# Each engine's order in the Q and K stage with a step of slack, and attention scores and maxima for two heads at a time

## The chip, the cores and the metric

The kernel runs on one core of a Trainium2 chip. The metric is the device time of one execution in microseconds (us), as the median of several runs. The core has five engines that run their own instruction streams in order and meet only at semaphores: the tensor engine (PE, with its weight loads PEld), VectorE (DVE), ScalarE (ACT), GpSimd (POOL) and SyncE (SP), which here only issues DMAs.

## The reference

Input are x (4 x 512 x 512), a context (4 x 512 x 256) and two gates. First a selective scan (Mamba-like) runs over the context, gated by the normalized x, and is added to x; then a transformer block with causal attention (16 heads of 32) and a mixture of experts (8, two per token, and a shared one) runs over the normalized sum and is added again. Everything is float32. What matters here, cut down:

```python
def step(state, xs):                      # the scan: 512 channels, 16 states each, 512 steps
    d_t, B_t, C_t, u_t = xs
    dA = jnp.exp(d_t[..., None] * A)
    state = state * dA + (d_t * u_t)[..., None] * B_t[:, None, :]
    y_t = jnp.einsum('ben,bn->be', state, C_t)
    return (state, y_t)
...
q = (h @ wq + bq); k = (h @ wk + bk); v = (h @ wv + bv)      # as 16 heads of 32
q, k = _rope(q, k)
scores = jnp.einsum('bqhd,bkhd->bhqk', q, k) * HEAD_DIM ** (-0.5)
attn = jax.nn.softmax(jnp.where(causal[None, None], scores, min), axis=-1)
ctx = jnp.einsum('bhqk,bkhd->bqhd', attn, v)
x = x + ctx @ wo
```

## The kernel before

The work goes in rounds, `round_(b, s)` on each engine, with b the batch whose attention runs and s = b + 1 the batch whose scan runs: a first round with the scan of batch 0 alone (to some 205 us), three rounds with both (to some 497, 793 and 1087 us), and a last one with the attention of batch 3 alone (to 1286 us). Then the experts' stage runs to the end; the change doesn't touch it.

**The scan.** It is cut into 64 blocks k of 128 channels x 512 positions: state n = k // 4, channel tile et = k % 4. GpSimd makes GB = DU x BB (`driven(k)`, four buffers), ScalarE the decay exp(A delta) in a PSUM bank (`decay(k)`), VectorE the scan itself (`scan(k)`), which writes row n into one of two buffers: `even_states` for even n, `xa` for odd n. So row n writes over row n - 2, and `scan(4n)` waits until the turns of all blocks up to 4n - 5 are done (`hT_ready`). The tensor engine turns a finished block of 128 positions (`turn_states(q)`, four transposes into a bank), and VectorE adds it, times C, to the output sum YA (`add_state(q)`). In the Q and K stage two banks take the turned states by turns, in the attention loop only HT0 does: there each turn waits for the sum before it.

**The Q and K stage** has eight steps m. Step m makes one of eight tiles of Q or K: `product` (twelve matmuls of 128x512, a product of split numbers) and `rotate` (the rope's swap, a matmul) on the tensor engine, `bias` on ScalarE, `rope_cos` on GpSimd (writes RC, two buffers), `rope_out` on VectorE (two operations, RS and then QK from RC and RS). Beside it two blocks of the scan go through in each step.

**The attention loop** has sixteen steps q: row tile i = q // 4, four heads m = q % 4, tiles 128 x W with W = 128 (i + 1). The tensor engine makes the scores of four heads one q ahead (`scores(q + 1)`), VectorE their negated maxima (`row_max`), ScalarE the exponentials (`probs`, one per head), the tensor engine transposes each (`turn`), ScalarE copies it out (`keep_turned`, PT), and `weigh(q)` multiplies with V behind a transpose of the inverse sums (`rib`). The three blocks of the scan k = 16 + 3q, k + 1, k + 2 go beside it, with three turned and summed states. `finish` (the product with wo, the second norm, the router) of row tile i - 1 is spread over the q of tile i.

All orders are written out by hand, in `round_` of each engine. One PSUM area SB of four banks holds the scores; the same banks are A[0] to A[3], which the rotation (A[0], A[1]), the turned states (A[2]) and the decays (A[3]) use in the Q and K stage.

## Time and profile before

| | |
|---|---|
| median of 3 runs | 2016.72 us (2014.46 to 2017.73) |
| the profiled execution | 2015.7 us, span 2013.9 us |
| mean granted clock of the tensor engine | 0.845 of full speed |
| busy: PE, DVE, ACT, POOL | 1560.5, 1174.1, 887.6, 808.3 us |
| chain that ended last, by engine | PE 51%, issue 18%, DVE 8%, POOL 7%, ACT 5% |

The profile is one execution of the program. Busy times are sums over the span, which has stages with different limits, so they are read stage by stage. In the chain of waits "issue" is time in which an engine waited for nothing that the profile shows. A matmul's own duration overlaps the next one's; the distance from start to start tells what it costs.

### The profile page before, as it was taken

What the parts mean: (1) busy time and instruction counts of PE and PEld (TensorE: products, weight loads), DVE (VectorE), ACT (ScalarE), POOL (GpSimd) and SP (SyncE); (2) the same over time, 40 slices, a digit from 0 to 9 for tenths busy, and PEclk for the clock granted to TensorE, in tenths of its full rate; (3) what the DMA queues carried; (4) which work ended last, traced back from release to release, by engine and by line L of the source; (5) the groups of instructions that cost most, each with busy time, mean ns of one, the idle gap of its engine ahead of it and who ended that gap; (6) DMA issues with size and microseconds to landing.
All of it is one profiled execution on the core that took longest, in us unless ns stands there. A gap on an engine that the chain in (4) does not pass through costs nothing.

```text
span 2013.9 us, 26645 instructions
## 1 busy us (share of the span) xinstructions
PE 1560.5 (77%) x9104; PEld 1196.1 (59%) x9104; DVE 1174.1 (58%) x1730; ACT 887.6 (44%) x1973; POOL 808.3 (40%) x809
## 2 busy tenths in 40 slices
PE   5345866776866777767776877789999999999994
PEld 2234543554544555544554644677878799999973
DVE  4779657777557777557775334233233365666545
ACT  5342624664524665515663256211111266666610
POOL 0685145443145542244542212123522265555544
PEclk8555975788985888986788878899999999999997
DMA  5521000112100112000112200542211187777564
GB/s 196 212 65 63 12 16 21 48 49 68 32 16 21 59 42 74 28 12 30 43 37 63 79 22 33 214 179 81 92 52 37 46 299 258 254 246 252 171 239 157
DMA packets 95109, 197.31 MB, mean 98 GB/s; under 512 B 9008, under 2 KB 25904, under 8 KB 91648
## 3 DMA queue, kind: packets, MB, share of 16 engines
q1 hardware_dynamic: 89856, 178.83, 25.8%
q0 software_dynamic: 5120, 16.78, 2.5%
q8 instruction: 74, 1.21, 0.2%
q14 instruction: 59, 0.48, 0.1%
HBM read 141.97 MB, written 53.61 MB: 97 GB/s over the span
## 4 chain that ended last, share of the span: by engine, by line
PE 51%; issue 18%; DVE 8%; POOL 7%; ACT 5%; DMA 0%; DVEq 0%; ACTq 0%; POOLq 0%; SPq 0%
PE scores L552 20%; PE bank L552 13%; PE bank L628 4%; PE scores L692 3%; PE bank L705 3%; DVE YA L1444 3%; POOL GB L1860 3%; PE bank L720 3%; ACT PT L1100 2%; POOL yab L2013 2%; ACT EX L1092 1%; PE scores L695 1%; DVE nm L1505 1%; PE bank L716 1%; PE bank L881 1%
## 5 line engine op out<-in xcount | busy, mean ns | idle before, releaser
L1860 POOL TENSOR_TENSOR GB<-DU,BB 128x512 f32<-128x512 f32 x256 | 324.2, 1290 | 48.8 <-DVE DL L1415 21.6
L1056 ACT ACTIVATE bank<-DL,aneg 128x512 f32<-128x512 f32 x200 | 138.0, 690 | 159.3 <-DVE xa L1434 94.1
L1100 ACT ACTIVATE PT<-bank 128x128 f32<-128x128 f32 (+3 forms) x256 | 111.0, 434 | 146.4 <-PE bank L705 143.1
L1444 DVE SCALAR_TENSOR_TENSOR YA<-bank,Ct,YA 128x512 f32<-128x512 f32 x208 | 153.1, 737 | 13.8 <-PE bank L628 10.8
L552 PE MATMUL scores<-xth,wgh 128*128 128x256 f32 x552 | 158.0, 286 | 2.2 <-DVE fa L1747 1.1
L628 PE MATMUL bank<-ident,xa 128*128 128x128 f32 x432 | 90.9, 350 | 85.9 <-DVE YA L1444 60.7
L628 PE MATMUL bank<-ident,even_states 128*128 128x128 f32 x400 | 81.7, 340 | 97.5 <-DVE even_states L1434 53.4
L552 PE MATMUL scores<-xth,wgl 128*128 128x256 f32 x552 | 156.1, 283 | 0.0
L552 PE MATMUL scores<-xtl,wgh 128*128 128x256 f32 x552 | 156.0, 283 | 0.0
L705 PE MATMUL bank<-ident,EX 128*128 128x128 f32 x640 | 133.1, 316 | 17.6 <-ACT PT L1100 15.8
L1092 ACT ACTIVATE EX<-scores,nm 128x128 f32<-128x128 f32 (+3 forms) x256 | 133.6, 523 | 23.6 <-DVE nm L1505 23.0
L1434 DVE TENSOR_TENSOR_SCAN xa<-bank,GB 128x512 f32<-128x512 f32 x100 | 121.9, 1219 | 17.9 <-ACT bank L1056 17.6
L1434 DVE TENSOR_TENSOR_SCAN even_states<-bank,GB 128x512 f32<-128x512 f32 x100 | 121.9, 1219 | 17.8 <-ACT bank L1056 17.7
L628 PEld LDWEIGHTS bank<-ident,even_states 128*128 128x128 f32 x400 | 56.6, 173 | 125.5 <-DVE even_states L1434 64.8
L628 PEld LDWEIGHTS bank<-ident,xa 128*128 128x128 f32 x432 | 63.7, 178 | 110.3 <-DVE YA L1444 61.0
L1985 POOL TENSOR_TENSOR fal<-fa,fah 128x512 fp32r<-128x512 f32 x36 | 46.5, 1290 | 200.3 <-ACT fah L1268 200.1
L552 PE MATMUL scores<-hah,wgh 128*128 128x512 f32 x320 | 125.6, 392 | 1.1 <-DVE lg L1535 1.1
L552 PE MATMUL scores<-hal,wgh 128*128 128x512 f32 x320 | 125.3, 392 | 0.0
L552 PE MATMUL scores<-hah,wgl 128*128 128x512 f32 x320 | 125.2, 391 | 0.0
L1968 POOL TENSOR_TENSOR wgl<-wgr,wgh 128x768 fp32r<-128x768 f32 x54 | 110.6, 2050 | 30.4 <-ACT wgh L1239 30.4
L1892 POOL TENSOR_TENSOR PT<-EX,rope 128x512 f32<-128x512 f32 x32 | 41.9, 1309 | 197.8 <-ACT EX L1084 197.8
L1505 DVE TENSOR_REDUCE nm<-scores 128x4 f32<-128x512 f32 (+3 forms) x64 | 95.3, 1489 | 34.4 <-PE scores L695 33.8
(250 smaller groups left out, 4108.4 us busy)
## 6 DMA issues: line engine op xcount, KB each, us to landing
wgr<-wffn_in SPq DMA_DIRECT2D x108, 384.0 KB, 6.3
wdr<-wffn_in SPq DMA_DIRECT2D x81, 256.0 KB, 3.4
BB<-b_scratch SPq DMA_DIRECT2D x64, 256.0 KB, 3.1
xg<-V SPq DMA_DIRECT2D x1, 11776.0 KB, 39.0
xr<-xg SPq DMA_DIRECT2D x23, 512.0 KB, 5.8
yg<-ysb SPq DMA_DIRECT2D x23, 512.0 KB, 6.3
hah<-hhd SPq DMA_DIRECT2D x5, 1024.0 KB, 6.0
hal<-hhd SPq DMA_DIRECT2D x5, 1024.0 KB, 8.3
```

The source lines that it names most:

```text
L552: mm = nc.tensor.matmul(out_, parts[a](k), rhs_parts[b](k), start=(k == 0 and j == 0), stop=(k == n - 1 and j == 2))
L628: mm = nc.tensor.transpose(into[:, et * P:(et + 1) * P], states(s, n)[:, et, tt * P:(tt + 1) * P], ident[:])
L692: nc.tensor.matmul(SB[:, a, 0:W], QK[r:r + HD, m, i * P:(i + 1) * P], QK[r:r + HD, 4 + m, 0:W], start=True, stop=False)
L705: mm = nc.tensor.transpose(turned_bank(b, v)[:, kb * P:(kb + 1) * P], EX[:, a, kb * P:(kb + 1) * P], ident[:])
L1056: nc.scalar.activation(into, DL[:, et, :], ACT.Exp, scale=aneg[:, et, n:n + 1]).then_inc(dA_ready, 1)
L1092: nc.scalar.activation(EX[:, a, 0:W], SB[:, a, 0:W], ACT.Exp, bias=nm[:, a:a + 1], accum_out=rs[:, q % 2, a:a + 1]).then_inc(ex_done, 1)
L1100: nc.scalar.activation(PT[:, a, 0:W], turned_bank(b, v)[:, 0:W], ACT.Copy).then_inc(pt_done, 1)
L1434: nc.vector.tensor_tensor_scan(states(s, n)[:, et, :], decay_bank(s, k)[0], GB[:, k % 4, :], 0.0, ALU.mult, ALU.add).then_inc(scan_done, 1)
L1444: nc.vector.scalar_tensor_tensor(YA[:, tt, :], state_bank(s, q)[0], Ct[:, tt, n:n + 1], YA[:, tt, :], ALU.mult, ALU.add).then_inc(y_acc, 1)
L1505: nc.vector.tensor_reduce(nm[:], SB[:, :, 0:W], AX.X, ALU.max, negate=True).then_inc(mx_done, 1)
L1860: nc.gpsimd.tensor_tensor(GB[:, k % 4, :], DU[:, et, :], BB[:, n % 2, :], ALU.mult).then_inc(gb_ready, 1)
L1968: nc.gpsimd.tensor_tensor(wgl[raw][:, c, :], wgr[raw][:, c * 2 * EW:(c + 1) * 2 * EW], wgh[raw][:, c, :].bitcast(f32), ALU.subtract).then_ ...
```

## The change

The numbers SL = 11 and NP = 2 NQ are new. In the Q and K stage:
- GpSimd makes the GB of blocks 0 and 1 first, and in step m those of 2m + 2 and 2m + 3 behind `rope_cos(m)` (2m and 2m + 1 before).
- VectorE runs `rope_out(m - 1)` at the end of step m, behind both scans (`rope_out(m)` between them before), and adds state k - 5 behind scan k (k - 4 before).
- The tensor engine puts `rotate(m - 1)` between the two turned states (ahead of both before) and turns eleven states in the stage (twelve before).

In the attention loop the scores and their maxima are made for two heads at a time: p = 2q + h. `scores(2q + 3)` stands where `scores(q + 1)` stood, `scores(2q + 4)` behind the third turned state of q. The turned states and their sums are one block later than before: 11 + 3q + a in q (12 + 3q + a before). The last one goes behind the loop.

```diff
@@ state_bank
-            if s == 0 or q < SQ - T4:
+            if s == 0 or q < SL:
                 return (HT0, A[2])[q % 2], q - 2
-            return HT0, q - 2 if q == SQ - T4 else q - 1
+            return HT0, q - 1
@@ tensor engine
-            def scores(b, q):
+            def scores(b, p):
+
+                q, h = divmod(p, 2)
                 i, m = quad(q)
                 W = P * (i + 1)
-                if q == 0:
+                if p == 0:
                     pe.wait_ge(v_done, T4 * b + T4)
                     pe.wait_ge(qk_done, 8 * b + 8)
-                    if b + 1 < B:
-                        pe.wait_ge(scan_done, NB * (b + 1) + SQ)
-                        pe.wait_ge(y_acc, NB * (b + 1) + SQ - T4)
-                at(pe, ex_done, UN * b + HG * q)
-                for a in range(HG):
+                if p == 1 and b + 1 < B:
+                    pe.wait_ge(scan_done, NB * (b + 1) + SQ)
+                    pe.wait_ge(y_acc, NB * (b + 1) + SL - 1)
+                at(pe, ex_done, UN * b + HG * (q - 1) + 2 * h + 2)
+                for a in (2 * h, 2 * h + 1):
...
                     if att:
                         product(b, m)
-                        if m:
-                            rotate(b, m - 1)
                     if scn and m >= 2:
                         turn_states(s, 2 * m - 4)
+                    if att and m:
+                        rotate(b, m - 1)
+                    if scn and 2 <= m < 7:
                         turn_states(s, 2 * m - 3)
                 if att:
                     rotate(b, 7)
                     scores(b, 0)
+                    scores(b, 1)
+                    scores(b, 2)
                 for q in range(NQ):
                     i, m = quad(q)
                     if att and q + 1 < NQ:
-                        scores(b, q + 1)
+                        scores(b, 2 * q + 3)
                     for a in range(HG):
+                        if att and a == 3 and q + 2 < NQ:
+                            scores(b, 2 * q + 4)
                         if att:
                             turn(b, HG * q + a)
                         if scn and a < SU:
-                            turn_states(s, SQ - T4 + SU * q + a)
+                            turn_states(s, SL + SU * q + a)
...
                 if scn:
+                    turn_states(s, NB - 5)
@@ ScalarE
-                act.wait_ge(mx_done, NQ * b + q + 1)
+                act.wait_ge(mx_done, NP * b + 2 * q + a // 2 + 1)
@@ VectorE
             def scan_out(s):
+                add_state(s, NB - 5)
...
-            def row_max(b, q):
+            def row_max(b, p):
+                q, h = divmod(p, 2)
                 W = P * (quad(q)[0] + 1)
-                dve.wait_ge(s_mm, NQ * b + q + 1)
-                nc.vector.tensor_reduce(nm[:], SB[:, :, 0:W], AX.X, ALU.max, negate=True).then_inc(mx_done, 1)
+                dve.wait_ge(s_mm, NP * b + p + 1)
+                nc.vector.tensor_reduce(nm[:, 2 * h:2 * h + 2], SB[:, 2 * h:2 * h + 2, 0:W], AX.X, ALU.max, negate=True
+                                        ).then_inc(mx_done, 1)
...
-                    if scn:
-                        scan_block(s, 2 * m)
-                    if att:
-                        rope_out(b, m)
-                    if scn:
-                        scan_block(s, 2 * m + 1)
+                    for k in (2 * m, 2 * m + 1):
+                        if scn:
+                            scan(s, k)
+                        if scn and k >= 5:
+                            add_state(s, k - 5)
+                    if att and m:
+                        rope_out(b, m - 1)
+                if att:
+                    rope_out(b, 7)
                 if att:
                     row_max(b, 0)
+                    row_max(b, 1)
+                    row_max(b, 2)
                     invert(b, 0)
...
                     if more:
-                        row_max(b, q + 1)
+                        row_max(b, 2 * q + 3)
                     if scn:
+                        add_state(s, k - 5)
+                        scan(s, k + 1)
                         add_state(s, k - 4)
-                        scan_block(s, k + 1)
                     if att and i and m != 1:
                         finish(b, i - 1, (1, 0, 2, 3)[m])
+                    if att and q + 2 < NQ:
+                        row_max(b, 2 * q + 4)
                     if scn:
-                        scan_block(s, k + 2)
+                        scan(s, k + 2)
+                        add_state(s, k - 3)
@@ GpSimd
+                if scn:
+                    driven(s, 0)
+                    driven(s, 1)
                 for m in range(8):
                     if att:
                         rope_cos(b, m)
                     if scn:
-                        driven(s, 2 * m)
-                        driven(s, 2 * m + 1)
-                if scn:
-                    driven(s, SQ)
-                    driven(s, SQ + 1)
+                        driven(s, 2 * m + 2)
+                        driven(s, 2 * m + 3)
```

VectorE at the start of the Q and K stage (round 0), before: even_states or xa is a scan, EX<-scores,rope and QK are the rope, YA a state's sum.

```order
L1434 SCALAR_TENSOR_TENSOR even_states<-scores,GB 128x512
L1495 SCALAR_TENSOR_TENSOR EX<-scores,rope 128x512
L1499 SCALAR_TENSOR_TENSOR QK<-PT,EX 128x512
L1434 SCALAR_TENSOR_TENSOR even_states<-bank7,GB 128x512
L1434 SCALAR_TENSOR_TENSOR even_states<-scores,GB 128x512
L1495 SCALAR_TENSOR_TENSOR EX<-scores,rope 128x512
L1499 SCALAR_TENSOR_TENSOR QK<-PT,EX 128x512
L1434 SCALAR_TENSOR_TENSOR even_states<-bank7,GB 128x512
L1434 SCALAR_TENSOR_TENSOR xa<-scores,GB 128x512
L1444 SCALAR_TENSOR_TENSOR YA<-bank6,Ct,YA 128x512
```

The same place in the changed kernel:

```order
L1444 SCALAR_TENSOR_TENSOR even_states<-scores,GB 128x512
L1444 SCALAR_TENSOR_TENSOR even_states<-bank7,GB 128x512
L1444 SCALAR_TENSOR_TENSOR even_states<-scores,GB 128x512
L1444 SCALAR_TENSOR_TENSOR even_states<-bank7,GB 128x512
L1501 SCALAR_TENSOR_TENSOR EX<-scores,rope 128x512
L1505 SCALAR_TENSOR_TENSOR QK<-PT,EX 128x512
L1444 SCALAR_TENSOR_TENSOR xa<-scores,GB 128x512
L1444 SCALAR_TENSOR_TENSOR xa<-bank7,GB 128x512
L1454 SCALAR_TENSOR_TENSOR YA<-bank6,Ct,YA 128x512
```

The rope of a tile has moved from between its step's scans to behind the next step's, and the first sum to behind scan 5.

VectorE in one q of the attention loop (q = 1, W = 128; nm is the maximum, ri the inverse, cn the context), before:

```order
L1434 SCALAR_TENSOR_TENSOR even_states<-bank7,GB 128x512
L1515 TENSOR_TENSOR cn<-bank4,rbs 128x128
L1505 TENSOR_REDUCE nm<-scores 128x4
L1444 SCALAR_TENSOR_TENSOR YA<-bank6,Ct,YA 128x512
L1434 SCALAR_TENSOR_TENSOR xa<-bank7,GB 128x512
L1444 SCALAR_TENSOR_TENSOR YA<-bank6,Ct,YA 128x512
L1434 SCALAR_TENSOR_TENSOR xa<-bank7,GB 128x512
L1444 SCALAR_TENSOR_TENSOR YA<-bank6,Ct,YA 128x512
L1510 RECIPROCAL ri<-rs 128x4
```

And in the changed kernel:

```order
L1444 SCALAR_TENSOR_TENSOR even_states<-bank7,GB 128x512
L1523 TENSOR_TENSOR cn<-bank4,rbs 128x128
L1512 TENSOR_REDUCE nm<-scores 128x2
L1454 SCALAR_TENSOR_TENSOR YA<-bank6,Ct,YA 128x512
L1444 SCALAR_TENSOR_TENSOR xa<-bank7,GB 128x512
L1454 SCALAR_TENSOR_TENSOR YA<-bank6,Ct,YA 128x512
L1512 TENSOR_REDUCE nm<-scores 128x2
L1444 SCALAR_TENSOR_TENSOR xa<-bank7,GB 128x512
L1454 SCALAR_TENSOR_TENSOR YA<-bank6,Ct,YA 128x512
L1518 RECIPROCAL ri<-rs 128x4
```

The one maximum of four heads has become two of two heads, and the second stands ahead of the q's third scan and sum. The first scan of xa here is block 20, the first of row n = 5: it writes over row 3, whose last block is now the second turned state of this q.

The tensor engine in the same q of the changed kernel (scores<-QK and maskb are the scores, bank5 the transposes of EX, bank6 the turned states, rib and V the sum over V):

```order
L696 MATMUL scores<-QK 128x128 x2
L699 MATMUL scores<-maskb,identb 128x128 x2
L709 MATMUL bank5<-ident,EX 128x128
L630 MATMUL bank6<-ident,xa 128x128 x4
L709 MATMUL bank5<-ident,EX 128x128
L630 MATMUL bank6<-ident,xa 128x128 x4
L709 MATMUL bank5<-ident,EX 128x128
L630 MATMUL bank6<-ident,even_states 128x128 x4
L696 MATMUL scores<-QK 128x128 x2
L699 MATMUL scores<-maskb,identb 128x128 x2
L709 MATMUL bank5<-ident,EX 128x128
L720 MATMUL bank4<-ident,rib 128x128
```

Before, the scores of four heads stood first in q; now two heads stand there and two behind the third turned state.

## Rows read from the trace of the kernel before

**Rows 1.** Sums by stage: window, length, busy us of each engine, granted clock, DMA.

```profile
545.00:605.00 60.00, 36.24 (x132) 24.90 (x130) 32.21 (x38) 13.92 (x21) 26.10 (x21) 0.82 0.05 14
605.00:791.00 186.00, 135.69 (x1016) 93.23 (x1016) 138.18 (x175) 105.90 (x289) 82.89 (x95) 0.75 0.16 49
```

**Rows 2.** Chain of waits, Q and K stage: start, us, what.

```profile
552.68 2.50 POOL GB L1860 x2
...
596.13 2.56 POOL GB L1860 x2
```

**Rows 3.** Timeline of one step: start, us, engine, line, operation, out<-in.

```profile
589.17 1.22 DVE L1434 TENSOR_TENSOR_SCAN even_states<-scores,GB 128x512 f32<-128x512 f32 x1 [3.35 <-POOL GB L1860]
590.31 0.73 DVE L1444 SCALAR_TENSOR_TENSOR YA<-bank,Ct,YA 128x512 f32<-128x512 f32 x1
...
590.95 0.68 DVE L1495 SCALAR_TENSOR_TENSOR EX<-scores,rope 128x512 f32<-128x512 f32 x1
591.66 0.69 DVE L1499 SCALAR_TENSOR_TENSOR QK<-PT,EX 128x512 f32<-128x512 f32 x1
592.27 1.22 DVE L1434 TENSOR_TENSOR_SCAN even_states<-bank,GB 128x512 f32<-128x512 f32 x1
...
593.52 0.69 ACT L1056 ACTIVATE bank<-DL,aneg 128x512 f32<-128x512 f32 x1 [2.41 <-DVE even_states L1434]
...
594.90 1.28 POOL L1892 TENSOR_TENSOR PT<-EX,rope 128x512 f32<-128x512 f32 x1 [4.53 <-ACT EX L1084]
```

**Rows 4.** Timeline: a rotation, a turned state; chain: a product.

```profile
599.04 1.02 PE L678 MATMUL scores<-EX,perm 128*128 128x512 f32 x2
...
599.90 0.60 PE L628 MATMUL bank<-ident,even_states 128*128 128x128 f32 x4
...
1123.77 2.75 PE bank L552 x12
```

**Rows 5.** Timeline of VectorE: the last sum of DL.

```profile
542.44 0.69 DVE L1415 TENSOR_TENSOR DL<-DL,GB 128x512 f32<-128x512 f32 x1
```

**Rows 6.** Timeline of rounds 3 and 0; line L1499: count, ns min/median/max.

```profile
1138.13 1.29 POOL L1892 TENSOR_TENSOR PT<-EX,rope 128x512 f32<-128x512 f32 x1 [2.31 <-ACT EX L1084]
...
1138.95 1.01 DVE L1499 SCALAR_TENSOR_TENSOR QK<-PT,EX 128x512 f32<-128x512 f32 x1
...
306.11 6.22 POOL L1860 TENSOR_TENSOR GB<-DU,BB 128x512 f32<-128x512 f32 x5
...
309.94 2.94 DVE L1499 SCALAR_TENSOR_TENSOR QK<-PT,EX 128x512 f32<-128x512 f32 x1
...
L1499 DVE SCALAR_TENSOR_TENSOR QK<-PT,EX x32: 691/693/2944, 249.2 to 1144.2; 128x512 f32<-128x512 f32 x32
```

**Rows 7.** Timeline of the tensor engine: the first scores.

```profile
612.82 0.81 PE L692 MATMUL scores<-QK 32*128 32x128 f32 x8 [7.09 <-DVE YA L1444]
```

**Rows 8.** Timeline: inverses turned, q = 0, 3, 15; thirteen left out.

```profile
623.91 0.47 PE L716 MATMUL bank<-ident,rib 128*128 128x128 f32 x1 [0.37 <-ACT PT L1100]
...
648.59 0.47 PE L716 MATMUL bank<-ident,rib 128*128 128x128 f32 x1 [0.37 <-ACT PT L1100]
...
778.45 0.43 PE L716 MATMUL bank<-ident,rib 128*128 128x128 f32 x1 [0.69 <-ACT PT L1100]
```

**Rows 9.** Chain of waits in q = 1: a turn, a sum.

```profile
628.32 1.10 PE bank L628 x4
...
629.52 0.76 DVE YA L1444
```

**Rows 10.** Groups by line, shapes apart: maxima (busy us, mean ns).

```profile
L1505 DVE TENSOR_REDUCE nm<-scores 128x4 f32<-128x2048 f32 x16 | 36.6, 2287 | 11.7 <-PE scores L695 11.7
...
L1505 DVE TENSOR_REDUCE nm<-scores 128x4 f32<-128x512 f32 x16 | 11.1, 692 | 8.6 <-PE scores L695 8.4
```

**Rows 11.** Chain of waits in round 3, W = 384: the maximum.

```profile
1218.40 1.77 DVE nm L1505
```

**Rows 12.** DMA issues of the page: count, KB each, us to landing.

```profile
BB<-b_scratch SPq DMA_DIRECT2D x64, 256.0 KB, 3.1
```

More of the change, by code:

```diff
@@ L34 @@
 SU = 3
+SL = 11
+NP = 2 * NQ
 MASKED = -3.0e38
@@ L693, in scores @@
                                      start=True, stop=False)
-                for a in range(HG):
+                for a in (2 * h, 2 * h + 1):
                     mm = nc.tensor.matmul(SB[:, a, W - P:W], identb[:], maskb[:], start=False, stop=True)
@@ L1445, in add_state @@
                                                ALU.mult, ALU.add).then_inc(y_acc, 1)
-            def scan_block(s, k):
-                scan(s, k)
-                if k >= T4:
-                    add_state(s, k - T4)
             def gate(s, tt):
```

## Prediction

> **What bounds the kernel now.** I read the sums by stage first. In one of the three rounds that hold both scan and attention, the Q and K stage takes 60 us with VectorE busy 32 of them and the tensor engine 36, and the attention loop 186 with 138 and 136 [rows 1]. No engine is full, so orders and waits set the time. Next the chain of waits: in the Q and K stage it comes back to GpSimd's pair of GB products once in each step m, and five steps last from 552.68 to 596.13, 8.69 each [rows 2]. The timeline of one step shows the ring [rows 3]. VectorE runs scan (589.17), sum, the two operations of the rope, scan (592.27); the second scan frees its bank for ScalarE's decay (593.52), behind which stands the bias of step m+1; that releases GpSimd's cosine product (594.90), behind which stand the GB products (596.13 in [rows 2]), for which VectorE's next scan waits. Only the written order ties these together: bias(m+1) stands behind decay(2m+3), and cosine(m+1) ahead of the GB products of the same step.
>
> **Q and K stage, in three rounds.** GpSimd now makes GB a step ahead, VectorE takes the rope a step later and adds each state one block later, and TensorE puts one turn between product and rotation. The ring of 8.69 opens, and what is left is each engine's own work in a step. VectorE, from start to start [rows 3]: scan 1.14, sum 0.64, scan 1.14, sum 0.64, rope 0.71 and 0.61, so 4.9. TensorE at full clock: product 2.75, rotation 0.86, two turns of 0.60 at most [rows 4], so 4.8. GpSimd: 1.23 + 2.56, so 3.8 [rows 2, 3]. About 5 a step, set by VectorE.
>
> One cost rises. The rope's last operation (QK<-PT,EX) has both its inputs in SBUF. Started during one cosine product it took 1.01 instead of 0.69; during five GB products in a row 2.94, until just after the last of them [rows 3, 6]. GpSimd now runs cosine, GB, GB without a gap in every step, so in my schedule a QK that falls into such a run waits for its end. Cosine(m+1) in its turn waits for QK(m-1), which keeps most of them apart. The schedule of one round, by hand from the rows: the last sum of DL starts at 542.44 and ends at 543.1 [rows 5]. GpSimd's first GB follows, loses some 0.5 to VectorE's last DU product (two SBUF inputs too) and ends at 545.0. Five GB and two cosines behind it, 1.26 each, end at 553.8; QK(0) waits for them and ends at 554.4. From there VectorE still has 12 scans (13.7), 11 sums (7.1) and 7 ropes (9.3), 30.1, and QK is held five times for 0.3 to 1.35, 2.9 together. QK(7) ends at 587.4 and the first scores can start; before, they start at 612.82, released by a sum of YA [rows 7]. **Gain 25.4 a round.** With no hold it is 29. With a hold as long as the worst row (2.94 - 0.69 = 2.25) in each of seven steps, 15.8 stands in place of 2.9, and it is 12.5. I take 25.4, since the median of all 32 is 0.69 [rows 6] and cosine cannot run ahead of QK by more than two.
>
> The Trainium skill, SBUF — State Buffer, "Who interferes with whom", says that a VectorE instruction with two SBUF inputs and a GpSimd one that reads SBUF exclude each other, and that the second fully blocks until the first finishes. The 1.01 row agrees with it; the 2.94 row goes further than one instruction. Held by one instruction only, QK(0) and QK(6) would end 1.2 to 1.3 sooner, and the time would be some 7 us lower.
>
> The loads of b rows (3.1 us to land [rows 12]) wait for the GB products of two rows before; they come earlier with them and have two steps in hand, so 0.
>
> **Attention loop, in three rounds.** Before, a q of the first four costs (648.59 - 623.91)/3 = 8.2, the next twelve 129.9 together [rows 8]. A q is paced by turn 1.10, sum 0.75, turn, sum, turn [rows 9], at half clock (the same four transposes took 0.60 [rows 4]); the scans run beside the turns. Three things add waits.
> (a) VectorE has row_max(2q+4) ahead of scan(k+2), and TensorE makes these scores only behind the third turn. The third scan no longer lies beside that turn: after it come half the scores (0.64), a maximum (0.43: widths differ by 0.53 for each 512 elements [rows 10]), scan 1.14, sum 0.75, inverse 0.15, scan 1.14, context 0.27, maximum 0.43, sum 0.7, turn, sum, turn (3.0): 8.7 against 8.2.
> (b) A state is turned one block later (SL = 11, where it was 12). scan(4n) writes over row n-2, so it waits for turn 4n-5. That was always a turn of the q before or one that a sum ahead had waited for. Now it is the first turn of the same q (q = 0, 4, 8, 12), the second (1, 5, 9, 13) or the third (2, 6, 10, 14, already in (a)). Price 0.7 to 1.1 for the second; 0 to 1.6 for the first, which has half the scores, a turn of EX, PT and the sum over V ahead of it.
> (c) Where a q also holds the product with wo (twelve matmuls, up to 2.75 as in [rows 4]), the third turn, its scores and the maximum stand behind it: about 1 more.
> Against these: the maximum ahead of the first sum is half as long, at 512 columns 1.2 instead of 2.29 [rows 10], and the first two exponentials of q+1 find theirs ready. My sums: entry 0.3, q 1 to 3 1.6 + 0.5 + 0.4, so +2.8; q 4 to 7 +2.8; q 8 to 11 +0.5; q 12 to 15 -1.0; one more turn behind the last sum over V +0.4. **Together +5.5 a round.** The ends: every wait at half clock +16; at full clock, hidden by the shorter maxima, -4. I take the value between, as the granted clock was 0.75 in this loop [rows 1].
>
> **Round 3, attention alone.** Its Q and K stage keeps its order. In the loop, a q whose chain held scores, the maximum (1.77 [rows 11]) and then four exponentials now has half the scores ahead, the rest before the fourth turn, and two exponentials that wait for nothing: 8.0 becomes 7.2 in the five q of that kind, and nothing where ScalarE's exponentials bound already. **-4**, between -10 and +3.
>
> **The first round, scan alone,** adds each state one block later; VectorE has the same operations and no wait: 0. The experts' stage is untouched: 0.
>
> **Sum.** 3 x (-25.4 + 5.5) - 4 = -63.7. On the profiled execution of 2015.7 (span 2013.9) that is 1952; the median of the runs lies 1.0 higher: 1953.
>
> **Rivals.**
> 1. The attention's new waits are covered, since the tensor engine runs more of it at full clock: -3 a round instead of +5.5, 3 x (-25.4 - 3) - 4 = -89, so 1927. For: with wide tiles VectorE's maximum led the chain, and it is halved. Against: the first q ran at half clock.
> 2. The holds or the waits come at their upper end. GpSimd is first every time: gain 12.5 instead of 25.4, 1953 + 39 = 1992. Or the waits cost +16 instead of +5.5: 1984. For: the 2.94 row. Against: cosine waits for the QK before last.
> 3. Slower than before: the tensor engine is granted 1.2 GHz through both stages. A step is then twice 4.8, so 9.6 against 8.69, no gain; and the loop costs +16: 2017 + 48 = 2065, anything from 2021 up. It decides once a step is over 6.7 (a gain under 16). Against: the old stage had 0.82 with the engine busy 36 of 60 us [rows 1]; it will be busy 4.8 of 5.
> 4. The ring opens but another one of the same length stands behind it, so the orders don't bring what they could: loops that I find take 4.2 (decay, bias, cosine, GB to the scan after next) and 4.3 (scan, sum, turn, product, turn, rotation, rope over two steps), both below 5. 2017 within 4.
>
> **How the numbers follow.** The forecast 1953 (1938 to 1968) has 50%; rival 1 18%; rival 2 24% (1968 to 2012); rival 3 5%; rival 4 3%. To hold 8 in 10 the range takes the forecast, rival 1 down to 1925 and rival 2 up to 1990. Faster by over 0.2% (about what a measurement can tell from no change) 92%, within it 3%, slower 5%.
>
> **What would show it.** GB pairs in the Q and K stage 5.0 to 5.6 apart, the granted clock above 0.9 there, the first scores some 45 us after the last sum of DL instead of 70, QK operations of 0.7 to 3 us; in the loop VectorE idle ahead of row_max for the scores and ahead of the first scan of a row for a turn, with q 1 near 9.8 and q 2 and 3 near 8.7. Wrong if the steps stay above 6.7, or if q 1 costs no more than q 2, or if the loop as a whole is longer by over 16.

## The result

The changed kernel takes 2034.43 us (median of 4 runs, 2032.09 to 2036.22), the kernel before 2015.59 beside it (4 runs, 2013.92 to 2017.73): ratio 1.0092, interval 1.0075 to 1.0110. It is slower by 19 us, where 1953 was forecast. The profiled execution has a span of 2034.4 us (2013.9 before) and a mean granted clock of 0.822 (0.845 before). One other execution of the kernel before, beside e1 to e4 below, took 2589.91 us at a granted clock of 0.543 and stands in no ratio.

Sums by stage, round 1 of the changed kernel. Columns as in [rows 1]: window, length, busy us of PE, PEld, DVE, ACT and POOL, granted clock, DMA. The first line is the Q and K stage, the second the attention loop:

```profile
540.00:588.00 48.00, 34.90 (x150) 24.35 (x150) 44.68 (x51) 19.99 (x31) 34.88 (x27) 0.96 0.08 23
588.00:785.00 197.00, 153.96 (x970) 101.53 (x970) 124.97 (x173) 104.69 (x287) 75.58 (x89) 0.68 0.12 37
```

The same stages of the kernel before, cut at its own first scores:

```profile
541.00:613.00 72.00, 39.64 (x144) 26.53 (x144) 40.94 (x49) 16.90 (x27) 34.66 (x27) 0.80 0.06 15
613.00:780.00 167.00, 123.83 (x956) 85.06 (x960) 123.84 (x155) 103.14 (x284) 75.50 (x88) 0.76 0.13 41
```

The Q and K stage lost 24 us and VectorE fills 93% of it. The loop grew by 30 us between these cuts, and so did the tensor engine's busy time in it: 154 against 124, with the clock at 0.68 against 0.76. VectorE's work in the loop is the same (125 and 124). So the gain came, and more than it went again in the loop.

Timeline around the end of the Q and K stage and the first scores (columns as in [rows 3]), to be set beside [rows 7]:

```profile
586.67 1.06 DVE L1505 SCALAR_TENSOR_TENSOR QK<-PT,EX 128x512 f32<-128x512 f32 x1
587.83 0.49 PE L696 MATMUL scores<-QK 32*128 32x128 f32 x4 [4.76 <-issue]
```

The inverses turned in q = 0, 3 and 15 of the same round, to be set beside [rows 8]:

```profile
600.38 0.47 PE L720 MATMUL bank<-ident,rib 128*128 128x128 f32 x1 [0.37 <-ACT PT L1110]
...
630.08 0.47 PE L720 MATMUL bank<-ident,rib 128*128 128x128 f32 x1 [0.37 <-ACT PT L1110]
...
782.08 0.33 PE L720 MATMUL bank<-ident,rib 128*128 128x128 f32 x1 [0.69 <-ACT PT L1110]
```

From q = 0 to q = 15 that is 181.7 us; before it was 154.5 [rows 8]. There is one such row for each q, so the distance between two of them is the price of a q. This table is worked out from all of them, in round 1 (for e1 and e6 too); the q meant is the later one:

| q | 1 | 2 | 3 | 4 | 5 | 6 | 7 | 8 | 9 | 10 | 11 | 12 | 13 | 14 | 15 | sum |
|---|---|---|---|---|---|---|---|---|---|---|---|---|---|---|---|---|
| before | 8.1 | 8.1 | 8.5 | 9.9 | 8.9 | 9.0 | 11.8 | 11.6 | 9.9 | 10.6 | 12.6 | 13.5 | 11.1 | 12.0 | 8.9 | 154.5 |
| after | 10.2 | 9.5 | 10.0 | 13.6 | 10.9 | 10.4 | 13.5 | 15.7 | 11.9 | 11.4 | 14.3 | 17.6 | 11.9 | 11.9 | 8.9 | 181.7 |
| e1, below | 9.1 | 7.5 | 8.5 | 14.1 | 9.7 | 9.0 | 11.6 | 17.2 | 10.8 | 10.6 | 12.3 | 18.5 | 12.0 | 12.4 | 8.9 | 172.1 |
| e6, below | 9.2 | 8.1 | 8.5 | 10.6 | 9.6 | 9.0 | 11.6 | 12.2 | 10.8 | 10.6 | 11.6 | 13.9 | 11.5 | 12.4 | 9.7 | 159.2 |

Over the whole kernel these rows give the account. The first inverse comes 23.5 us earlier (325.53 to 302.07), the stretches from a round's last inverse to the next round's first are shorter by 26.0 and 24.0 (142.4 to 116.4, 142.2 to 118.2): -73.5. The loops of the three rounds are longer by 25.9, 27.2 and 30.1, that of round 3 by 7.7 (115.4 to 123.1): +90.9. With +0.6 between rounds 2 and 3 the last inverse comes 18 us later (1267.1 to 1285.3). The rest of the kernel, which has the same instructions, takes 749.1 in this execution against 746.8.

### The profile page after: what moved, and what is told of

The parts are those of the page before. It is cut to its first block, busy times and chain, and to the rows that moved or that the text cites. A ratio compares the mean times of both kernels' runs of the same rounds, so it can differ in the third digit from the quotient of the medians.

```text
span 2034.4 us, 26709 instructions
## 1 busy us (share of the span) xinstructions
PE 1653.3 (81%) x9104; PEld 1238.7 (61%) x9104; DVE 1183.8 (58%) x1794; ACT 891.7 (44%) x1973; POOL 809.6 (40%) x809
## 4 chain that ended last, share of the span: by engine, by line
PE 60%; issue 11%; DVE 10%; ACT 4%; POOL 4%; DMA 0%; DVEq 0%; ACTq 0%; SPq 0%; POOLq 0%
PE scores L554 22%; PE bank L554 14%; PE scores L696 6%; PE bank L630 5%; DVE YA L1454 3%; PE bank L709 3%; PE bank L724 3%; PE scores L699 2%; ACT PT L1110 2%; POOL yab L2030 2%; DVE even_states L1444 1%; PE bank L720 1%; DVE xa L1444 1%; PE bank L891 1%; ACT EX L1102 1%
## 5 line engine op out<-in xcount | busy, mean ns | idle before, releaser
L1512 DVE TENSOR_REDUCE nm<-scores 128x2 f32<-128x256 f32 (+3 forms) x128 | 105.1, 821 | 129.3 <-PE scores L699 129.2
L696 PE MATMUL scores<-QK 32*128 32x256 f32 (+3 forms) x512 | 146.6, 661 | 23.7 <-issue 11.6
L1454 DVE SCALAR_TENSOR_TENSOR YA<-bank,Ct,YA 128x512 f32<-128x512 f32 x211 | 154.7, 734 | 13.9 <-PE bank L630 11.8
L630 PE MATMUL bank<-ident,even_states 128*128 128x128 f32 x412 | 89.3, 356 | 89.8 <-DVE YA L1454 64.0
L554 PE MATMUL scores<-xtl,wgh 128*128 128x256 f32 x552 | 156.0, 283 | 0.0
L709 PE MATMUL bank<-ident,EX 128*128 128x128 f32 x640 | 145.4, 340 | 8.6 <-ACT PT L1110 8.4
L630 PE MATMUL bank<-ident,xa 128*128 128x128 f32 x432 | 95.6, 365 | 57.3 <-DVE YA L1454 56.8
L630 PEld LDWEIGHTS bank<-ident,even_states 128*128 128x128 f32 x412 | 62.1, 181 | 112.1 <-DVE YA L1454 43.0
L2002 POOL TENSOR_TENSOR fal<-fa,fah 128x512 fp32r<-128x512 f32 x36 | 46.5, 1290 | 200.2 <-ACT fah L1278 200.0
L630 PEld LDWEIGHTS bank<-ident,xa 128*128 128x128 f32 x432 | 68.2, 187 | 78.6 <-DVE YA L1454 41.6
```

The costliest lines, as they stand in the source:

```text
L554: mm = nc.tensor.matmul(out_, parts[a](k), rhs_parts[b](k), start=(k == 0 and j == 0), stop=(k == n - 1 and j == 2))
L630: mm = nc.tensor.transpose(into[:, et * P:(et + 1) * P], states(s, n)[:, et, tt * P:(tt + 1) * P], ident[:])
L696: nc.tensor.matmul(SB[:, a, 0:W], QK[r:r + HD, m, i * P:(i + 1) * P], QK[r:r + HD, 4 + m, 0:W], start=True, stop=False)
L709: mm = nc.tensor.transpose(turned_bank(b, v)[:, kb * P:(kb + 1) * P], EX[:, a, kb * P:(kb + 1) * P], ident[:])
L1454: nc.vector.scalar_tensor_tensor(YA[:, tt, :], state_bank(s, q)[0], Ct[:, tt, n:n + 1], YA[:, tt, :], ALU.mult, ALU.add).then_inc(y_acc, 1)
L1512: nc.vector.tensor_reduce(nm[:, 2 * h:2 * h + 2], SB[:, 2 * h:2 * h + 2, 0:W], AX.X, ALU.max, negate=True).then_inc(mx_done, 1)
```

## The experiments

Three things stand mixed in the change: the orders of the Q and K stage, one block less between a turned state and the scan that writes over it (SL = 11, twelve before), and scores and maxima for two heads at a time. The first four kernels take them apart. The kernel before beside them took 2017.9, 2017.1 and 2016.0 us in the three groups of runs (e1 to e4; e5, e6, e8, e9; e7, e10, e11).

**e1: the stage's orders and SL = 11, four heads at a time.** Against the changed kernel:

```diff
-                        scores(b, 2 * q + 3)
+                        scores(b, q + 1)
...
-                        if att and a == 3 and q + 2 < NQ:
-                            scores(b, 2 * q + 4)
...
-                        row_max(b, 2 * q + 3)
+                        row_max(b, q + 1)
...
-                    if att and q + 2 < NQ:
-                        row_max(b, 2 * q + 4)
```

> The changed kernel with scores and maxima of four heads at a time again, at their old places; the new orders of the Q and K stage and the turned states one block later (SL = 11) stay. Theory A (two heads' scores occupy the tensor engine as long as four, since four heads' matmuls on 32 rows each run side by side; the pairs cost the attention loop its 26 to 30 us a round): the loop from the first to the last inverse turned goes back to within 5 to 9 of the old 156, that is the row waits alone, and the time is about 1965. Theory B (the waits of scan(4n) for a turn of the same q are the loss, at 1.0 to 2 us in half of the q): the loop stays at 170 or more and the time is 2000 or more.

Measured: 1998.50 us, ratio 0.9911 (0.9894 to 0.9929). The loops of the three rounds with both take 171.4, 172.1 and 173.2 us, so it is theory B that fits, the waits for a turn. Theory A, which had put nearly all of the loss on the scores, is out as to size by 33 us.

**e2: e1 with twelve states turned in the stage.** The attention loop is word for word that of the kernel before:

```diff
-SL = 11
+SL = 12
...
+                if scn:
+                    add_state(s, 11)
                 if att:
                     rope_out(b, 7)
...
-                        add_state(s, k - 5)
-                        scan(s, k + 1)
                         add_state(s, k - 4)
+                        scan(s, k + 1)
+                        add_state(s, k - 3)
```

> As the run before, and twelve turned states in the Q and K stage again (the twelfth sum between the last two ropes), so that the attention loop is that of the kernel before, word for word. Both theories: the loop takes 152 to 156 a round again, the Q and K stage keeps its gain of 24 less 0.7 for the sum, and the time is 2015.6 - 3 x 23.5 = 1945. If it is above 1965, the gain of the stage is given back by the attention loop for another reason than these orders (the state in which it starts).

Measured: 1938.32 us, ratio 0.9614 (0.9597 to 0.9631), 7 less than expected. The orders of the Q and K stage are worth 79.6 us alone, 26.5 a round. The one block of lead costs 60.2 (e1 against e2), some 19 in each of these loops (172.1 against 152.5 in round 1) and 3.9 ahead of the first inverse.

**e3: the kernel before with scores and maxima for two heads**, placed as in the changed kernel, and nothing else:

```diff
-                        scores(b, q + 1)
+                        scores(b, 2 * q + 3)
                     for a in range(HG):
+                        if att and a == 3 and q + 2 < NQ:
+                            scores(b, 2 * q + 4)
...
-                        row_max(b, q + 1)
+                        row_max(b, 2 * q + 3)
...
+                    if att and q + 2 < NQ:
+                        row_max(b, 2 * q + 4)
                     if scn:
                         scan_block(s, k + 2)
```

> The kernel before with the scores and maxima for two heads at a time alone (places as in the changed kernel; Q and K stage and turned states as before). Theory A: the loop takes 18 to 25 more in each of three rounds and 8 in the last, the time is 2015.6 + 60 to 85, about 2085. Theory B: only the third scan behind the second maximum, 0.6 in the first q and nothing later: about 2020, at most 2030.

Measured: 2055.27 us, ratio 1.0186 (1.0168 to 1.0204). Two heads at a time cost 37 us on their own, which neither theory had: A said 60 to 85, B at most 15. The loops are longer by 10.9, 10.8 and 15.6, that of round 3 by 7.7.

**e4: the kernel before, its score matmuls written in two halves in their old place.** The same matmuls, waits and maxima; only the order of the twelve records of one group changes:

```diff
-                for a in range(HG):
-                    r = HD * a
-                    nc.tensor.matmul(SB[:, a, 0:W], ...)
-                for a in range(HG):
-                    mm = nc.tensor.matmul(SB[:, a, W - P:W], identb[:], maskb[:], start=False, stop=True)
+                for h in range(2):
+                    for a in (2 * h, 2 * h + 1):
+                        r = HD * a
+                        nc.tensor.matmul(SB[:, a, 0:W], ...)
+                    for a in (2 * h, 2 * h + 1):
+                        mm = nc.tensor.matmul(SB[:, a, W - P:W], identb[:], maskb[:], start=False, stop=True)
```

> The kernel before; only the sequence of matmuls within the scores of four heads differs: heads 0 and 1, their masks, heads 2 and 3, their masks. Same matmuls, same waits, same places. Theory A: the scores of a q take twice 0.8 to 2.0 instead of once, about 1.2 more on average for 64 q and nearly all on the path: 2060 to 2095. Theory B, and any explanation by waits: no change, within 4 of 2015.6.

Measured: 2085.06 us, ratio 1.0338 (1.0316 to 1.0360): +67 for a change of order alone, as theory A said (2060 to 2095), where theory B had no change. Timeline of the tensor engine at 512 columns, first the kernel before, at half and at full clock (start, us; x8 are eight records, two for each of four heads):

```profile
734.79 2.09 PE L692 MATMUL scores<-QK 32*128 32x512 f32 x8
736.81 0.61 PE L695 MATMUL scores<-maskb,identb 128*128 128x128 bf16 x4
...
747.68 1.14 PE L692 MATMUL scores<-QK 32*128 32x512 f32 x8
748.75 0.40 PE L695 MATMUL scores<-maskb,identb 128*128 128x128 bf16 x4
```

The same in e4:

```profile
771.45 1.13 PE L693 MATMUL scores<-QK 32*128 32x512 f32 x4
772.51 0.28 PE L696 MATMUL scores<-maskb,identb 128*128 128x128 bf16 x2
...
782.32 2.08 PE L693 MATMUL scores<-QK 32*128 32x512 f32 x4
784.33 0.39 PE L696 MATMUL scores<-maskb,identb 128*128 128x128 bf16 x2
784.65 2.08 PE L693 MATMUL scores<-QK 32*128 32x512 f32 x4
786.66 0.39 PE L696 MATMUL scores<-maskb,identb 128*128 128x128 bf16 x2
```

The granted clock is 0.50 around the rows of 2.08 and 2.09 us and 1.00 around those of 1.13 and 1.14. At half clock four heads take 2.09 us and two heads 2.08. A head has 32 rows ("32*128" in the row), and the kernel takes those of head a from partition 32a on, so the four stand in different groups of rows, and they run together. Two of them alone are no sooner done.

**e7: one head at a time**, score and mask, score and mask:

```diff
                     nc.tensor.matmul(SB[:, a, 0:W], ...)
-                for a in range(HG):
                     mm = nc.tensor.matmul(SB[:, a, W - P:W], identb[:], maskb[:], start=False, stop=True)
```

> The kernel before, with the score matmuls and the mask of one head at a time: score 0, mask 0, score 1, mask 1 and so on. The same matmuls, waits and maxima. In e4 (heads 0 and 1 with their masks, then heads 2 and 3) the kernel before went from 2018 to 2085, +67. Theory: a group of score matmuls takes as long as one matmul, however many heads of 32 rows lie side by side in it, up to four. Four groups are two more than in e4, so another 2 x 67: near 2218, and the first of the four scores to the last mask twice as long as in e4. Rival: two heads side by side are already served one after the other, and what e4 cost is a fixed price of the change between scores and masks: with three changes more instead of one, 67 for each gives the same 2218, but then the trace shows scores of e4's pairs that start as far apart as in e7. If only a fixed latency is paid once, 2085 to 2100.

Measured: 2264.34 us, ratio 1.1247 (1.1219 to 1.1275), +181 and +248 against e4 and before. Timeline of the tensor engine at full clock:

```profile
867.50 1.12 PE L692 MATMUL scores<-QK 32*128 32x512 f32 x2
868.56 0.23 PE L694 MATMUL scores<-maskb,identb 128*128 128x128 bf16 x1
868.72 1.12 PE L692 MATMUL scores<-QK 32*128 32x512 f32 x2
```

One head takes 1.12, two 1.13, four 1.14: the time belongs to the group and not to the heads, and the rival of this expectation (two heads already served one after the other) is out. The busy time of all score matmuls, summed over the four widths of the view by line and shape, is 76 us before, 151 in e4 and 312 in e7, that of the masks 34, 46 and 70. That is +87 and +272 of busy time for +67 and +248 of time. The theory's size was short, 2264 for some 2218: a further group costs the engine much the same (87 us in e4, 272 / 3 = 91 in e7). Of the 87 in e4 20 don't show in the time, of the 272 in e7 24; a likely reason is that they lay in time that the engine waited anyway and that there was little more of it to fill, which no run tests.

The Trainium skill, TensorE: Matmul & The Clock Gate, "Part 3: Packing small matmuls — row/col tiling", says that small matmuls on different groups of 32 rows run at the same time, and gives 3.07 times the speed for four of them at 512 columns. These rows agree that they run together, and the factor by them is higher: 4 x 1.12 in e7 against 1.14 before, 3.9.

**e5: the changed kernel with twelve states turned in the stage** (the edit of e2 on top of the change).

> The changed kernel with twelve turned states in the Q and K stage and the attention's turned states and sums where they were before (lead of 12); the scores and maxima for two heads stay. Theory C (the two losses, pairs +37 and one block less of lead +60, are separate): 1938 + 37 = 1975. Theory D (they are one wait seen twice, scan and maximum behind the same turn): the pairs cost the less when the lead is back, under 1960, or the more, over 1990.

Measured: 1984.81 us, ratio 0.9839 (0.9822 to 0.9855), 10 above what theory C said and under the 1990 of theory D, so it settles neither. The lead is worth 49.6 here, and two heads at a time cost 46.5 (e5 against e2). So the three terms are -79.6, +60.2 and +46.5; they sum to +27 where +19 was measured, so the two costs overlap by 8. Two heads at a time cost 37 on the old stage (e3), 46.5 here, and 36 with the shorter lead (the changed kernel against e1).

**e10: e5 with VectorE's third scan ahead of the second maximum.**

```diff
+                    if scn:
+                        scan(s, k + 2)
                     if att and q + 2 < NQ:
                         row_max(b, 2 * q + 4)
                     if scn:
-                        scan(s, k + 2)
                         add_state(s, k - 2)
```

> The changed kernel with twelve turned states in the stage (e5, 1984.8 us), and with VectorE's third scan of a q ahead of row_max(2q+4) instead of behind it. It prices term (a) of the prediction, the third scan that lies no longer beside the turn of EX. Theory: what two heads at a time cost (e5 against e2, +46) is the doubled time of the score matmuls on the tensor engine, so VectorE's order moves little: 1975 to 1988. Rival: term (a) as predicted, 0.5 a q in twelve q of three rounds, some 18, is a real part of the 46: 1967 or less.

Measured: 1960.11 us, ratio 0.9722 (0.9705 to 0.9740). The rival had it: 24.7 of the 46.5 come back by VectorE's order alone, with as many score matmuls as in e5 (139 us busy in both). VectorE's waits for scores fall from 120.6 to 81.7 us in all. In q = 11 and 12 of round 1, for one, 14.6 and 14.1 became 11.3 and 14.3. What stays, 22 against e2, goes with 74 us more of score and mask matmuls (139 and 45 against 76 and 33); what shorter maxima and earlier exponentials give back of them was not taken apart. Round 3, which has no scans, didn't move: 123.0, against 123.2 in e5 and 115.5 in e2.

**e6: e1 with the first scan of a row out of the way.** In q = 0, 4, 8 and 12, where `scan(4n)` waits for a turn of the same q, it stands behind the context, the maximum and the first sum, and ScalarE copies the context out ahead of the decay:

```diff
-                    if scn:
+                    if scn and k % T4:
                         scan(s, k)
...
                         add_state(s, k - 5)
+                        if k % T4 == 0:
+                            scan(s, k)
                         scan(s, k + 1)
```

> As e1_stage_only (scores of four heads, turned states one block later, 1998), but in q = 0, 4, 8, 12 VectorE takes scan(4n), the one that waits for a turn of the same q, behind context, maximum and the first sum, and ScalarE takes its copy of the context ahead of the decay that waits for that scan. Same work, same lead. Theory E (the price of 4 to 5 us in q = 4, 8, 12 is what was queued behind the waiting scan: the context, hence the product with wo, and this product at half clock after the idle time): most of it goes, these q fall by 2.5 to 4 each, the time is 1965 to 1975. Theory F (the late turn is itself the length of the ring there): these q keep their 13.6, 16.4 and 18.1, and the time stays within 5 of 1998.

Measured: 1962.98 us, ratio 0.9730 (0.9714 to 0.9746), 35.5 of the 60.2 back, 2 more than theory E said. By the table above q = 4, 8 and 12 fall from 14.1, 17.2 and 18.5 to 10.6, 12.2 and 13.9; the others change by less than 1. What happened in them is seen in e1's timeline of q = 8, round 1:

```profile
664.56 0.95 PE L630 MATMUL bank<-ident,even_states 128*128 128x128 f32 x4
665.54 1.22 DVE L1438 TENSOR_TENSOR_SCAN even_states<-bank,GB 128x512 f32<-128x512 f32 x1 [3.99 <-PE bank L630]
666.68 0.27 DVE L1515 TENSOR_TENSOR cn<-bank,rbs 128x128 f32<-128x128 f32 x1
666.87 1.75 DVE L1505 TENSOR_REDUCE nm<-scores 128x4 f32<-128x1536 f32 x1
667.43 0.29 ACT L1115 ACTIVATE cth<-cn 128x128 fp32r<-128x128 f32 x1
667.80 0.46 POOL L1908 TENSOR_TENSOR ctl<-cn,cth 128x128 fp32r<-128x128 f32 x1 [5.77 <-ACT cth L1115]
668.53 0.74 DVE L1448 SCALAR_TENSOR_TENSOR YA<-bank,Ct,YA 128x512 f32<-128x512 f32 x1
669.42 1.09 PE L630 MATMUL bank<-ident,xa 128*128 128x128 f32 x4 [3.46 <-DVE YA L1448]
```

The scan waits 3.99 us for the first turn of its own q. Behind it on VectorE stand the context, the maximum and the sum that frees the bank, so the tensor engine waits 3.46 for its second turn, with the wo product behind that. And it comes out of that wait at half clock, as the sums over three stretches of e1 show (columns as in [rows 1]: full clock up to 668.60, half clock in the end of the wait and in the product):

```profile
665.30:668.60 3.30, 0.66 (x5) 0.31 (x3) 3.06 (x4) 1.29 (x3) 0.80 (x2) 1.00 0.00 0
668.70:670.50 1.80, 1.08 (x5) 1.11 (x6) 1.70 (x2) 0.69 (x3) 1.80 (x2) 0.50 0.01 5
670.50:675.40 4.90, 4.90 (x13) 3.66 (x12) 0.75 (x1) 1.22 (x3) 0.22 (x1) 0.50 0.16 52
```

The chain of waits of e1 has the product, then that of the kernel before at the same place:

```profile
670.50 5.12 PE bank L554 x12
```

```profile
694.97 2.75 PE bank L552 x12
```

The twelve matmuls take 5.12 instead of 2.75, 0.63 for a single one instead of 0.39. Those of q = 4 and 12 take 4.34 and 4.70 there, where the kernel before has 2.78 and 2.76. In e6 the product of q = 4 is back at 2.76, and those of q = 8 and 12 are off the chain. e6 moves context, maximum, sum and ScalarE's copy together, so it doesn't tell their shares.

**e8: e2 with each maximum in two halves**, scores of four heads together and the first sum between the halves.

```diff
-                        row_max(b, q + 1)
+                        row_max(b, q + 1, 0)
                     if scn:
                         add_state(s, k - 4)
+                    if more:
+                        row_max(b, q + 1, 1)
+                    if scn:
```

> As e2_stage_lead12 (1938), with the scores of four heads together but the maxima in two operations of two heads, the first sum between them, so that ScalarE's first two exponentials don't wait for the second maximum. If waiting for the whole maximum costs the attention loop what the chain shows (1.2 to 2.3 at a time in wide q), 64 q gain up to 0.5 each on average: 1915 to 1930. If VectorE is what bounds the wide q, the extra 0.17 of each second operation shows: 1938 to 1950.

Measured: 1931.43 us, ratio 0.9567 (0.9549 to 0.9585), 7 less than e2, between the two ranges expected. The loop of round 3 falls from 115.5 to 111.9; those beside a scan do not gain (155.7, 155.5, 156.8 against 152.5, 152.5, 154.8). So the traces do not place these 7 us: the profiled execution of e8 is the slowest of its four (1937.41) and that of e2 the fastest (1933.75).

**e9: e2 with the rope's first result left in PSUM.** RS goes back into the bank that it is read from, so the rope's last operation has one input in SBUF instead of two; the next rotation into the bank waits for that operation.

```diff
-                    pe.wait_ge(rope_s, 8 * b + m - 1)
+                    pe.wait_ge(qk_done, 8 * b + m - 1)
...
-                nc.vector.scalar_tensor_tensor(RS[:, m % 2, :], A[m % 2][:], f, rope[:, 1, :],
+                nc.vector.scalar_tensor_tensor(A[m % 2][:], A[m % 2][:], f, rope[:, 1, :],
...
-                nc.vector.scalar_tensor_tensor(QK[:, m, :], RC[:, m % 2, :], f, RS[:, m % 2, :],
+                nc.vector.scalar_tensor_tensor(QK[:, m, :], RC[:, m % 2, :], f, A[m % 2][:],
```

> As e2_stage_lead12 (1938), with the rope's first result written back into its PSUM bank instead of SBUF, so that the second operation (QK) has one input in SBUF and one in PSUM. Same number of operations and elements. Theory G (QK is held by GpSimd for its second SBUF input): every QK takes 0.69 to 0.75 in this kernel though GpSimd works just the same, the stage is shorter by the holds of some 2.5 us in each of three rounds, and the time about 1931. Theory H (something else about the crowded stage lengthens it): QK still shows 1.0 to 2.4, and the time stays at 1938.

Measured: 1926.58 us, ratio 0.9553 (0.9537 to 0.9569), 11.7 less than e2. The rope's last operation by its line (count, ns least, median, most), changed kernel, e2, e9:

```profile
L1505 DVE SCALAR_TENSOR_TENSOR QK<-PT,EX x32: 691/1019/2386, 254.8 to 1153.8; 128x512 f32<-128x512 f32 x32
```

```profile
L1497 DVE SCALAR_TENSOR_TENSOR QK<-PT,EX x32: 691/1019/1781, 252.7 to 1060.4; 128x512 f32<-128x512 f32 x32
```

```profile
L1497 DVE SCALAR_TENSOR_TENSOR QK<-PT,scores x32: 686/689/690, 253.6 to 1051.4; 128x512 f32<-128x512 f32 x32
```

With one input in PSUM no operation is held, as theory G said. The mean fell from 1065 to 688 ns, and 32 x 0.377 = 12.1 us is as much as the gain. That each hold was time on the path isn't shown by that: theory G said 1931, and between the two traces 5.2 us lie in the stretches ahead of the loops (first inverse 297.82 to 295.32, then 2.0, 0.0 and 0.7) and 4.0 in the loops.

**e11: e9 with halves in round 3 alone**, one directly behind the other:

```diff
-                        row_max(b, q + 1)
+                        for h in (0, 1) if s == B else (None,):
+                            row_max(b, q + 1, h)
```

> The kernel with the rope in its PSUM bank (e9, 1926.6 us), with the maxima of four heads made as two operations of two heads, one directly behind the other, in the last round alone (attention without a scan). With halves in every round the loop of the last round took 111.9 instead of 115.5 us, and those beside a scan 155.7 instead of 152.5 (e8 against e2). There the first sum stood between the halves; in the last round there is no sum. Theory: the gain is that ScalarE starts two exponentials after half of the maximum (1.2 instead of 2.29 us at 512 columns), so it is in full here: -3.6, 1923, and the loop of the last round near 112. Rival: the gain in e8 came from clock or placement and not from the halves; then 1926 to 1928 and a loop of 115.

Measured: 1921.49 us, ratio 0.9530 (0.9510 to 0.9550), near the 1923 of the theory. Its last loop takes 111.6, against 115.4 in e9. The order of e9 and e11 is not settled by their intervals, but the loop by itself is as in e8. A higher clock is not the reason: the granted clock over this loop is 0.742 in e11 and 0.744 in e8, against 0.766 in e9 and 0.769 in e2. But the size is open. e1 and e6 have the last loop of the kernel before, maxima of four heads and all, and take 112.9 for it at a granted clock of 0.787. Against these the halves gain 1.0 to 1.3. It is the fastest of these kernels, 4.7% below before.

## Where the prediction was right and where it failed

**The Q and K stage was right.** The step was to be about 5 us; GpSimd's cosine and GB runs in round 1 start 4.8 apart on average (549.16 to 582.95 for seven steps, single ones 3.7 to 5.9; 5.0 to 5.6 was said), at a granted clock of 0.96, where over 0.9 was to be seen. QK(7) was put at an end of 587.4 and ends at 587.7; that this fits so closely is in part luck, as the last sum of DL, from which the schedule counts, starts at 544.12 and not at 542.44. From there to the first scores it takes 43.7, where 45 was said. The gain was to be 25.4 a round; e2 measures 26.5. The hold of QK was to add 2.9 a round; five of the eight operations of round 1 were held, by 0.28 to 1.69, 3.6 in sum. The longest one started inside a run of two GB products and ended just behind the second, as the 2.94 row had it:

```profile
552.82 2.55 POOL L1877 TENSOR_TENSOR GB<-DU,BB 128x512 f32<-128x512 f32 x2
553.54 2.38 DVE L1505 SCALAR_TENSOR_TENSOR QK<-PT,EX 128x512 f32<-128x512 f32 x1
```

The step from a ring to each engine's own sum of work held.

**What failed is the loop's +5.5 a round,** where 25.9 to 30.1 came. Two terms of it are at fault, and by size the second is the larger: 50 to 60 us for the shorter lead (e5 and e1), 36 to 47 for two heads at a time.

**First failed step: "half the scores (0.64)".** Two heads were priced as half of four, and the second group as no extra work at all. The view by line and shape of the changed kernel (busy us, mean ns of one):

```profile
L696 PE MATMUL scores<-QK 32*128 32x512 f32 x128 | 46.7, 813 | 1.8 <-ACT EX L1102 1.5
L699 PE MATMUL scores<-maskb,identb 128*128 128x128 bf16 x256 | 45.5, 274 | 0.0
```

The same rows of the kernel before:

```profile
L692 PE MATMUL scores<-QK 32*128 32x512 f32 x128 | 24.6, 848 | 0.0
L695 PE MATMUL scores<-maskb,identb 128*128 128x128 bf16 x256 | 33.8, 275 | 0.0
```

The same 128 records of 0.8 us make 24.6 us before, so 4.4 of them run at a time on average; 46.7 after, so 2.2 do. With one head at a time (e7) it is 1.1. The other three widths read alike, 51.4 to 99.8. With the masks (33.8 to 45.5 in all widths) it is 82 us of new work on the tensor engine, 20 a round, where the sum had none. The mark stood in the "32*128" of [rows 7], where eight records take 0.81 us together, and 128 x 848 ns = 108 us against 24.6 busy would have said it before the run.

**Its consequences.** Term (a), the third scan behind the second maximum, was right in kind and too small: 24.7 us in all or 8.2 a round (e10), where 0.5 a q in twelve q make 6, and its maximum comes later still by the doubled scores. VectorE's waits for scores, before and after (us in all, times, longest):

```profile
DVE nm L1505 <- PE scores L695: 33.8, 34, 1.9
```

```profile
DVE nm L1512 <- PE scores L699: 129.2, 81, 3.4
```

The gain counted against it was sized well and did not pay: a maximum of two heads at 512 columns takes 1.22 (1.2 said, [rows 10]) and at 128 columns 0.42 (0.43 said). In round 3, where it was all that moved, -4 was said and +7.7 came. Maxima in halves shorten that loop once the scores stay together (e8, e11), by 1.0 to 3.9 as one takes e1 or e9 beside them: right in kind, its size open, and eaten by the scores.

**Second failed step: (b), "0 to 1.6 for the first".** The wait of `scan(4n)` for the second turn was put at 0.7 to 1.1 and measures 0.5 to 1.3 at q = 1, 5, 9 and 13 (e1 9.1, 9.7, 10.8 and 12.0 in round 1, e2 8.1, 9.2, 10.0 and 10.7). That for the first turn measures 4.0 to 5.6 in round 1: 14.1, 17.2 and 18.5 against 10.1, 11.6 and 13.5 in e2. Only the waiting scan was priced. Not named was what stands behind it on VectorE: the context (behind it ScalarE's and GpSimd's operations on it, cth and ctl, and the wo product), the maximum (behind it the exponentials), and the sum that frees the only bank of turned states. e6 gets 35.5 us back by moving just these ahead of the scan.

**The clock.** Of the price of 4.0, 5.6 and 5.0 in q = 4, 8 and 12 the wo product takes 1.6, 2.4 and 1.9 (4.34, 5.12 and 4.70 in e1), which the sum had at full clock, 2.75, throughout. The end "every wait at half clock, +16" was near in kind, but the loops were longer by 26 to 30.

**The rivals.** By its number, 2034, the result falls to rival 3 (2021 and up), with 5% on it, but only the number fits. Its condition, a step over 6.7, was not met (4.8), and its cause was wrong: the clock was not at half through both stages, but higher than before in the first (0.96 for 0.80) and lower in the loop (0.68 for 0.76). Rival 2 had the loop's waits at their upper end, +16 a round, and named the right place; it fell short by 10 to 14 a round. That an order which is harmless for time on VectorE could double work on the tensor engine was in no rival. "Wrong if the loop as a whole is longer by over 16" is what came true.

**Open.** Why halves of a maximum bring nothing beside a scan (e8) was not taken apart. One kernel's executions differ by up to 10 us (e2: 1933.75 to 1941.32, e11: 1917.93 to 1927.46), and the loops beside a scan that have the order of the kernel before take 151.7 to 156.0 in the traces of before, e2, e9 and e11. So prices by trace of 4 us or less a loop are not sure; those by medians are.

## What to carry over

Before cutting a group of matmuls with few rows in two, multiply its count by its mean duration and compare with the busy time of the view. Where the product is a multiple of it and the rows show few rows each ("32*128"), they run side by side, and half of them cost as much as all; here it was 4.4 times. A product that is only somewhat larger doesn't say so: the records of matmuls on all 128 rows overlap too (the masks 256 x 275 ns = 70 us against 33.8 busy), so look at the length of one group in the timeline as well. When a wait is moved earlier on an in-order engine, price what is queued behind the waiting instruction up to the first thing another engine needs, and price the other engine's next work at the clock it will have after idling. And of a change of several parts, run each by itself. Here one part was worth 4%, and the two others took more than that away.

## What the runs showed of the hardware

Score matmuls of 32 rows in different row groups: 1.12 us for one head, 1.13 for two, 1.14 for four at 512 columns and full clock, 2.08 for two and 2.09 for four at half clock. In e1 the granted clock fell from 1.00 to 0.50 during a wait of the tensor engine of 3.46 us, and the twelve matmuls of the product behind it came at 0.43 from start to start, the first apart, instead of 0.23 at full clock. A VectorE operation with both inputs in SBUF was held up to 1.7 us by GpSimd's runs (2.386 instead of 0.689); the same operation with one input in PSUM was never held, 686 to 690 ns in 32 of 32.
